# Two graph blocks on one core: the order of instructions at the front, seams and end, and grouped products

## The reference, cut to what matters

```python
h = jnp.maximum(_layernorm(x, axis=-1), 0.0)
x = x + _L0_gnn_ref(h, adj, adj, W_sa, a_sa, W_gcnb, b_gcnb, Wa, ba, Wb, bb)
h = jnp.maximum(_layernorm(x, axis=-1), 0.0)
x = x + _L1_gnn_ref(h, adj, W_stack)

# _L0_gnn_ref(x, ...): one layer
attn_a = sigmoid(concatenate([adj_a @ x, x], axis=1) @ Wa.T + ba)
attn_b = sigmoid(concatenate([adj_b @ x, x], axis=1) @ Wb.T + bb)
h = x @ W_sa
scores = (h @ a_sa[0, :Hd])[:, None] + (h @ a_sa[0, Hd:])[None, :]
e = jnp.where(adj_a != 0, jnp.exp(-leaky_relu(scores, 0.01)), 0.0)
x_a = (e / (jnp.sum(e, axis=1, keepdims=True) + 1e-05)) @ h
x_b = adj_b @ (x @ W_gcnb) + b_gcnb
return sigmoid(attn_a * x_a + attn_b * x_b)

# _L1_gnn_ref(x, ...): two layers of
Wh, Ws = jnp.split(x @ W, 2, axis=-1)
scores = Wh @ Ws.T
a = softmax(scores, axis=-1) * adj
x = leaky_relu(a @ Wh + x, 0.01)
```

## Time and profile before

| what | value |
|---|---|
| median of 3 runs | 1569.0 us (1568.11 to 1570.0) |
| the profiled execution | 1568.53 us |
| its span in the profile | 1566.7 us |
| granted clock of PE, mean | 1.00 |
| instructions | 34636 |
| PE busy | 1533.8 us (98%), 12826 matmuls |
| DVE, ACT, POOL busy | 1130.7 (72%), 1068.2 (68%), 983.9 us (63%) |
| memory traffic | 167.83 MB, mean 107 GB/s |

### The profile page before, as it was taken

One profiled execution on the slowest core, in us unless ns is written; L12 is line 12 of the kernel. 1 busy time (PEld: TensorE's weight loads), 2 busy tenths in 40 slices (PEclk: granted clock), 3 DMA queues, 4 the chain that ended last, 5 costly groups with the idle time before them and its releaser, 6 DMA issues.

```text
span 1566.7 us, 34636 instructions
## 1 busy us (share of the span) xinstructions
PE 1533.8 (98%) x12826; PEld 1524.1 (97%) x12826; DVE 1130.7 (72%) x2119; ACT 1068.2 (68%) x2081; POOL 983.9 (63%) x886
## 2 busy tenths in 40 slices
PE   6999999999999999999999999999999999999998
PEld 5999999999999999999999999999999999999997
DVE  7667666676675677777777777766777777777774
ACT  5689899899984566666666666646666666666666
POOL 4312222222210488888888888847888888888885
PEclk9999999999999999999999999999999999999999
DMA  4354444544440134343433435522443333334343
GB/s 162 65 101 122 116 119 117 149 117 120 116 101 28 42 92 106 107 109 99 107 107 107 111 105 174 183 62 81 104 105 104 104 105 105 104 105 105 105 108 106
DMA packets 98423, 167.83 MB, mean 107 GB/s; under 512 B 15951, under 2 KB 28878, under 8 KB 97998
## 3 DMA queue, kind: packets, MB, share of 16 engines
q1 hardware_dynamic: 70208, 117.75, 27.3%
q0 software_dynamic: 24336, 44.31, 12.0%
q10 hardware_dynamic: 3710, 3.56, 0.7%
HBM read 152.44 MB, written 13.14 MB: 106 GB/s over the span
## 4 chain that ended last, share of the span: by engine, by line
PE 88%; issue 4%; DVE 3%; DMA 2%; POOL 2%; ACT 1%; SPq 0%; DVEq 0%; POOLq 0%; ACTq 0%
PE PS L1349 32%; PE PS L1562 9%; PE PS L1565 9%; PE PS L1564 9%; PE PS L1426 5%; PE PS L1423 5%; PE PS L1425 5%; PE PS L1424 5%; PE PS L1422 5%; POOL FR L541 1%; DMA STGT<-adjt 1%; DMA ROW<-rec_scratch 1%; DMA rec_scratch<-COL 1%; POOL X L534 1%; DVE AF L1158 0%
## 5 line engine op out<-in xcount | busy, mean ns | idle before, releaser
L541 POOL TENSOR_TENSOR FR<-AF,FR 128x512 fp32r<-128x512 f32 x338 | 451.3, 1335 | 124.4 <-ACT FR L752 118.6
L1349 PE MATMUL PS<-FR,RB 128*128 128x256 f32 x3900 | 513.9, 281 | 1.8 <-ACT X L706 1.7
L1349 PEld LDWEIGHTS PS<-FR,RB 128*128 128x128 f32 x3900 | 481.7, 188 | 3.1 <-ACT X L706 3.0
L534 POOL TENSOR_TENSOR X<-X,ROW 128x512 f32<-128x512 f32 x283 | 369.2, 1305 | 81.9 <-ACT ROW L762 81.9
L1562 PE MATMUL PS<-FR,RA 128*128 128x256 f32 x1300 | 370.7, 285 | 3.2 <-POOL FR L541 3.2
L1565 PE MATMUL PS<-FR,RA 128*128 128x256 f32 x1300 | 365.0, 281 | 0.0
L1564 PE MATMUL PS<-FR,RA 128*128 128x256 f32 x1300 | 364.4, 280 | 0.0
L481 POOL DMA_DIRECT2D STGT<-adjt x169 | 91.3, 540 | 298.0 <-PE PS L1426 295.9
L1158 DVE TENSOR_TENSOR AF<-PS,AJ 128x512 f32<-128x512 f32 x338 | 231.1, 684 | 56.1 <-ACT PS L718 46.1
L706 ACT ACTIVATE X<-PS 128x512 f32<-128x512 f32 x272 | 162.5, 597 | 158.8 <-DVE AF L1090 151.4
L1090 DVE TENSOR_TENSOR AF<-PS,AF 128x512 f32<-128x512 f32 x286 | 196.4, 687 | 101.0 <-PE PS L1349 98.6
(11 more groups left out here) (175 smaller groups left out, 2408.1 us busy)
## 6 DMA issues: line engine op xcount, KB each, us to landing
AJ<-adjt SPq DMA_DIRECT2D x338, 256.0 KB, 2.7
STGT<-adjt POOLq DMA_DIRECT2D x169, 256.0 KB, 3.0
xt_scratch<-ROW SPq DMA_DIRECT2D x12, 512.0 KB, 2.6
RB<-xt_scratch SPq DMA_DIRECT2D x12, 512.0 KB, 5.3
x_scratch<-X ACTq DMA_DIRECT2D x13, 256.0 KB, 2.2
ROW<-x_scratch SPq DMA_DIRECT2D x13, 256.0 KB, 3.2
out<-ROW SPq DMA_DIRECT2D x12, 256.0 KB, 3.4
ROW<-rec_scratch SPq DMA_DIRECT2D x22, 128.0 KB, 3.8
```

Of the source, the lines that this page charges most:

```text
L534: nc.gpsimd.tensor_tensor(slot, slot, MB.unsqueeze(1).broadcast_to([P, 2, 256]), ALU.subtract)\
L541: nc.gpsimd.tensor_tensor(LO[g % 2], WA[g % 2], HI[g % 3].bitcast(F32), ALU.subtract)\
L1349: last = nc.tensor.matmul(out, stationary(a, k), moving(b, k), start=(k == 0 and i == 0), stop=(k == K - 1 and i == 2))
```

## The change

It does the following, with names as in the code.

1. unit0: the 20 products come in three groups, eight of adj behind stage_full, eight of e_hi behind hi_done, four of e_lo behind lo_done. weigh and weigh_last: eight products of the high part behind hi_d, four of the low part behind alo_d.
2. Front: transpose0(p+1) runs between products_g(p) and products_h(p) on PE, with new bank turns; ACT, DVE and POOL follow; DVE runs transposed_low(0) before variances, and mask0 before g_low. N_LATE is 27: ACT runs high0 before exp0 in units 14 to 26 too.
3. Seam 1: wh(2) runs before project_q(0) on PE, ACT and DVE; DVE's xt_low(12) comes one step later.
4. The W2 casts move from step 154 to steps 159 and 160.
5. Block 11 leaves NEAR: its reciprocal goes through memory. The layer-2 inputs of blocks 11 and 12 are written in place, so that one store and one load of 512 KB fewer are made.
6. Seam 2: wh(13) to wh(25) use other PSUM banks (WH2_BANK), their evictions on ACT and DVE come a step later (EV_AT), and turn_max(13) comes before the scores.
7. End: block 24's reciprocal is kept and used two steps after its end.

```diff
-N_LATE = UNITS + 1
+N_LATE = 2 * UNITS + 1
+EV_AT |= {182: (13,), 183: (14,), 184: (15, 16, 17, 18, 19, 20), 185: (21,), 186: (22,), 187: (23, 24), 188: (25,)}
+WH2_BANK = (5, 0, 1, 5, 0, 1, 2, 3, 5, 2, 3, 5, 2)
 WH_AT |= {181: (13,), 182: (14,), 183: (15,), 184: (16, 17, 18, 19, 20, 21), 185: (22,), 186: (23, 24), 187: (25,)}
+W2_AT = 159
-NEAR = (PAIRS - 2, PAIRS - 1, LB - 1)
+NEAR = (PAIRS - 1, LB - 1)
+FAR_X2 = PAIRS - 2
-R_END = {v + 3 * (b not in NEAR): b for v, b in A_END.items()}
+R_END = {v + (0 if b == PAIRS - 1 else 2 if b == LB - 1 else 3): b for v, b in A_END.items()}
...
         def turn(pr, i):
-            return 5 * pr + i + 1 if i else max(5 * pr - 4, 0)
+            return 5 * pr + (0, 1, 2, 4, 5)[i] if i else max(5 * pr - 2, 0)
...
                 if S_END.get(v - 2) is not None:
                     keep_max(S_END[v - 2])
-                if A_END.get(v - 1) in NEAR and v - 1 != LAST1:
-                    keep_rec(A_END[v - 1])
-                if x is not None and x < GL:
+                if x is not None and x < GL and x != CH:
                     exponent(x)
                 if e is not None:
                     evict(e)
+                if x == CH:
+                    exponent(x)
                 if x is not None:
                     high(x)
...
-                if v == 154:
-                    dve.wait_ge(w_hi, 4)
+                if v == W2_AT:
+                    dve.wait_ge(w_hi, 3)
                     nc.vector.tensor_tensor(WX[:, 1, :, D:2 * D], MS, WX[:, 0, :, D:2 * D].bitcast(F32),
                                             ALU.subtract).then_inc(wx_ready, 1)
+                if v == W2_AT + 1:
+                    dve.wait_ge(w_hi, 4)
                     nc.vector.tensor_tensor(WX[:, 1, :, 0:D], WRAW1[:, 1, :, 0:D], WX[:, 0, :, 0:D].bitcast(F32),
                                             ALU.subtract).then_inc(wx_ready, 1)
...
             variances(0, 0, 2, 1)
             scales(0, 0, 2)
             normalise(0)
...
             dve.wait_ge(x_in[1], 16)
+            statistics(2, 4)
             statistics(4, 6)
+            transposed_low(0)
             variances(1, 2, 6, 3)
-            transposed_low(0)
             scales(1, 2, 6)
             normalise(1)
...
             xt_low(11)
             wh_low(1)
             post_x1(PAIRS - 1)
+            wh_low(2)
             q_low(0)
             post_norm(PAIRS - 1)
-            wh_low(2)
             post_scales(PAIRS - 1)
             wh_low(3)
             wh_low(4)
...
-                if v == X12_AT:
+                if v == X12_AT + 1:
                     xt_low(PAIRS - 1)
...
+                tiles = [(h, jj, (2 * jj + h) * P) for h in range(2) for jj in range(2)]
+                pe.wait_ge(stage_full[n % NSTG], 16 * (n // NSTG + 1))
+                for h, jj, i0 in tiles:
+                    j, adj, a_to = 2 * u + jj, STG[n % NSTG][:, i0:i0 + P], PS[:, acc(pr) + 2 + h, :]
+                    nc.tensor.matmul(a_to[:, 0:GX], adj, G[:, j, 0:GX], start=(j == 0), stop=False)
+                    nc.tensor.matmul(a_to[:, 0:GX], adj, G[:, j, GX:2 * GX], start=False, stop=(j == T - 1))
+                pe.wait_ge(hi_done, n + 1)
+                for h, jj, i0 in tiles:
+                    j, e_hi, e_to = 2 * u + jj, FR[:, ah(n), i0:i0 + P], PS[:, acc(pr) + h, :]
+                    nc.tensor.matmul(e_to[:, 0:GX], e_hi, RA[:, j, 0:GX], start=(j == 0), stop=False)
+                    nc.tensor.matmul(e_to[:, 0:D], e_hi, RA[:, j, GX:GX + D], start=False, stop=False)
                 pe.wait_ge(lo_done, n + 1)
...
             for p in range(PAIRS):
-                if 1 <= p < PAIRS - 1:
-                    transpose0(p + 1)
                 pe.wait_ge(htlo_done, p + 1)
                 products_g(p)
-                if p == 0:
-                    transpose0(1)
-                    pe.wait_ge(w_ready, 1)
                 if p == 1:
                     turn_left()
+                if p < PAIRS - 1:
+                    transpose0(p + 1)
+                if p == 0:
+                    pe.wait_ge(w_ready, 1)
                 products_h(p)
...
+                pe.wait_ge(hi_d, g + 1)
+                tiles = [(2 * u + h, d, h * 256) for h in range(2) for d in range(K)]
+                for j, d, i0 in tiles:
+                    hi, to = HI[g % 3][:, i0:i0 + 256], PS[:, 4 + b % 2, d * 256:(d + 1) * 256]
+                    nc.tensor.matmul(to, RA[:, j, d * P:(d + 1) * P], hi, start=(j == 0 and d == 0), stop=False,
+                                     skip_group_check=True)
+                    nc.tensor.matmul(to, RA[:, j, D + d * P:D + (d + 1) * P], hi, start=False, stop=False,
+                                     skip_group_check=True)
                 pe.wait_ge(alo_d, g + 1)
...
-                        nc.tensor.matmul(to, w_hi_, hi, start=(u == 0 and h == 0 and d == 0), stop=False,
-                                         skip_group_check=True)
-                        nc.tensor.matmul(to, w_hi_, lo, start=False, stop=False, skip_group_check=True)
-                        last = nc.tensor.matmul(to, w_lo_, hi, start=False, stop=final, skip_group_check=True)
+                for j, d, i0 in tiles:
+                    lo, to = LO[g % 2][:, i0:i0 + 256], PS[:, 4 + b % 2, d * 256:(d + 1) * 256]
+                    last = nc.tensor.matmul(to, RA[:, j, d * P:(d + 1) * P], lo, start=False, stop=(j == T - 1),
+                                            skip_group_check=True)
...
             project_wh(0)
             transpose_x(11)
             project_wh(1)
+            project_wh(2)
             project_q(0)
-            for n in range(2, 6):
+            for n in range(3, 6):
                 project_wh(n)
```

175 lines of the change are left out of this document (83 added, 92 removed).

## The result

The changed kernel takes 1554.67 us at the median of four runs (1553.12 to 1556.08), the kernel before 1568.55 in the runs beside it. The ratio is 0.9916, with a 95% interval of 0.9904 to 0.9928: 13.9 us or 0.84% faster. One execution of e12 took 2744.93 us at a mean granted clock of 0.79 and is left out of its median.

A forecast was written before the change was run, and what follows sets the result against it. PE bounds the kernel, busy 1533.8 of 1566.7 us, so only some 33 us of idling can return. Terms sum to 12.1: 1568.5 - 12.1 = 1556.4, plus 0.5 for the median, 1557; forecast range 1552.5 to 1560.5 (chance 0.55).

The forecast's parts named there:

- Regrouped products: Units and weighs: broken w_hi pairs cost 0, the 676 added waits 0.3 us of loss, ends 0 and 1.7.
- The rule weighed there: Skill's rule that one weight load can serve many products; by it, breaking a pair would cost a load's visible part.
- Front: 0 to about 90 us: g(0) starts earlier, but both orders are level by unit 2; 0, ends -1.5 and +2.
- Units 11 to 16: Late stage load near 102 us: 16 products run before low0(15) is done; 2.0 us gained, upper end 3.6, lower 1.3.
- Seam 1: wh(5) still waits for wh_low(3): 0, ends 0 and 2.1; xt_low(12) a step later gives 0.8, ends 0 and 1.1.
- Weighs that wait for POOL: Four block ends: eight products ahead let POOL's low part come 0.95 us later; 2.6 us gained, ends 1.4 and 3.0.
- W2 casts: Moved to steps 159 and 160, one each: stalls of 0.45 and 0.27 us go; 0.7 gained, ends 0 and 0.7.
- Seam 2: 1030.66 to 1068.96 us: exponents and highs first, evictions later, no stall above 0.3; 5.5 us gained, ends 3.5 and 6.0.
- End: Before 1539.42 us: weighted(24) behind two masks returns about half of 1.8; 0.8 us gained, ends 0.3 and 1.8.
- More: Rival: front's 2, both seam stalls (2.1) and full 3.6 of units 11 to 16 come too; 17.8 us, 1551; chance 0.14.
- The slower one: Rival: breaking 1300 weigh pairs costs; decides from 9.3 ns a pair, at twice that 1581 us; chance 0.07.
- less: Rival: seam 2 gives half (2.8), units 11 to 16 1.3, block ends 1.4; 6.1 us, 1563; chance 0.17.

The follow-up runs named there:

- e12: Changed kernel with old front, wh_low(3) ahead of post_scales, the left-score store cut in two, and the row-maximum fold as a one-operand reduction: 1551.0 us.
- e3: Changed kernel with the front's order and bank turns of before: 1554.8 us, ratio 0.9921 to the kernel before.
- e10: Changed kernel with N_LATE back at 14, so ACT runs exponent before high in units 14 to 26: 1554.83 us, ratio 0.992.
- e6: Changed kernel with weigh and weigh_last in the old order of products behind the low part: 1554.69 us, ratio 0.9921.
- e7: Kernel before with seam 2's part alone (banks, later evictions, turn_max of block 13 first, block 12's reciprocal later): 1562.09 us, ratio 0.997.
- e5: Changed kernel with unit0's 20 products in the old order behind the low part: 1558.88 us, ratio 0.9949.
- e11: Kernel before with the product groups of unit0, weigh and weigh_last alone: 1562.26 us, ratio 0.9963.
- e9: Changed kernel with one more store of left scores (1536 packets of 4 bytes) at unit 60: 1556.03 us in one run.

## Why the prediction was right, and where it wasn't

The forecast was 12.1 us of gain and 1557; measured were 13.9 by the medians and 12.4 between the profiles, inside the forecast's own range. That the total is so near is in part luck. The changed kernel's profile holds 1.55 us at the lower clock and 1.4 us of a long fold, neither of which was in the sum; without them it would have gained about 15 where 12.1 was forecast (the profiles of e3 and e10, which have neither, are 15.1 and 14.9 us under that of before). The block ends were put too high, units 11 to 16, the rest of the first layer and the end too low, and these errors have opposite signs. Point by point:

**Bound.** Right: all that was gained are idle times of PE, at an unchanged price of a product.

**Regrouped products.** The sum had 0 for the pairs and 0.3 for the waits; second-layer groups cost 0.4 to 0.9 in all (0.44 in weighs 170 to 321, nothing in 0 to 150; e6, e7 and the kernels with groups), inside the ends. The rule weighed there doesn't hold here: in the timeline of before, from 1100 to 1500 us, the distance from L1562 to L1564 (same stationary) is 118 ns at the median of 528, and 118 from L1564 to L1565 (new stationary) at that of 529. (The mean of the first is 123.1, since 31 of them, each the first pair behind a turn of a block's end, are 200 to 205 ns long; the new order has 30 such distances from L1575 to L1577.) A repeated stationary is not cheaper. In the first layer the groups gained 0.8 us in 130 units, which no step had; why is open, the runs show only that it comes and goes with the order in unit0.

**Front.** The step gave 0. It costs 1.1 us at unit 10 (e3), and the sum came out right only because the late load swallowed that. I had followed the chain to unit 0 but not the later ones, where the two orders do not level.

**Units 11 to 16.** 2.0 forecast, 1.9 and 2.1 in e5 and e11. The other 1.2 of the 3.1 measured is the front's lateness, counted here instead of there: e3, with the old front, takes 18.72 us from unit 10 to 17.

**Seam 1.** Right: q(0)'s wait goes and wh(5) waits for wh_low(3) instead; 53.7 us in both orders, 0.6 less than before for xt_low(12). The lower clock of some executions, 1.55 us, was in no step.

**Weighs that wait for POOL.** The mis-sized term: 2.6 forecast. Restoring the old order gives 1.97 of stalls back there, of which 1.1 are in seam 2, and so 0.9 for block ends. Only the first of the four places, at 534 to 537, is there in every kernel without groups in weigh. The ones at 740 to 744 and at 976 to 979 are absent from e6 and e7, which have no groups either; ahead of both the trip of the reciprocal through memory was the slowest in the trace of before, 10.3 and 10.1 us (in e7 8.5 and 9.4), which fits, but no run parts it from other causes. (The 0.47 at 969 in e6 is another weigh, 146, behind the moved W2 cast.) The one at 1010 to 1013 stays in e7 and is gone in e6, so that another edit of the change removes it (the W2 casts or block 11; the runs don't part them). And I had costed nothing for what PE's earlier start does to others: with the groups PE and DVE run some 0.5 us further ahead of POOL, so that at block 12 the fold starts inside a POOL instruction. In all ten profiles with grouped weighs and the two-operand fold it has 0.64 to 0.66 us of that instruction ahead of it, and takes 0.92 us in five and 3.42 to 3.44 in the other five; in the three without (before, e6, e7) it starts 0.11 to 0.14 us before the instruction's end and takes 0.41. Two more folds, near 752 in e11 (3.42) and near 755 in e5 (0.92), start 0.64 us before an end as well. The numbers fit a fold that waits: 0.92 is the 0.64 that is left and 0.28, and 3.42 is that and two POOL instructions of 1.25 us from start to start. The Trainium skill ("SBUF — State Buffer", section "SBUF: two separate sides") says that a VectorE operation with two SBUF inputs and a GpSimd operation that reads SBUF exclude each other for the whole instruction. For the fold, the W2 casts (below) and e12 the traces agree; that a waiting fold can lose to the next two POOL instructions as well is measured, not stated there. Not every POOL instruction holds DVE back so: in the first layer low0, with two operands in SBUF, starts inside POOL's root of the layer norm with 0.66 us of it left, eleven times in the trace of before, and takes its usual time:

```profile
119.92 1.15 POOL L486 TENSOR_TENSOR LNT<-LNT,COL 128x2 f32<-128x2 f32 x1 [1.92 <-DVE LNT L905]
120.41 0.68 DVE L967 TENSOR_TENSOR FR<-AF,FR 128x512 fp32r<-128x512 f32 x1
```

What parts the two (the root's 128x2 elements, or its kind) no run shows. Each long fold costs PE about 1.4 us (in the changed kernel 1.08 at L1629 and 0.28 at the turn back).

**W2 casts.** 0.7 forecast, 0.4 measured. The 1.78 us of the second cast is a like case: two operands in SBUF. It is not a matter of the step: at 159 and 160 the two casts take 1.74 and 1.36 us, as they start with 1.19 and 0.81 us of a POOL instruction left, 0.55 us more than that each time, and the POOL instruction behind takes 1.77 in place of 1.3. The first of the two in the changed kernel:

```profile
959.78 1.32 POOL L546 TENSOR_TENSOR FR<-AF,FR 128x512 fp32r<-128x512 f32 x1
959.91 1.74 DVE L1328 TENSOR_TENSOR WX<-ROW,WX 128x512 fp32r<-128x512 f32 x1 [0.63 <-ACT WX L880]
961.04 1.77 POOL L539 TENSOR_TENSOR X<-X,ROW 128x512 f32<-128x512 f32 x1
```

**Seam 2.** 5.5 forecast, 6.0 measured, of them 5.1 by the order and banks alone (e7). The loss itself was 0.2 larger than the 6.0 that the prediction counted, since it took 266 full-size products for 264. The replay found no stall, and there is none. The rival in which half of it comes falls.

**End.** 0.8 forecast, 1.9 measured. Of it 0.4 is the groups' (34.45 in e11 against 34.84; 33.40 in e6 against 32.97), and 1.5 the order's: the term was mis-sized, since I kept weighted(24) ahead of a mask that row_exponent needs. In the new order three masks stand ahead of it, and PE's last transposes wait 0.17.

**Rivals.** "More" came partly true, by the groups' 0.9 in the first layer and the end, not by the front and seam 1 that it named. The slower one, broken pairs, is at most 0.7 ns a pair against the 9.3 from which it decides, 13 times too small. In "less" the parts named add up to 6.1 only if seam 1's 0.8 and the 0.3 for the waits are left out; with them it is 6.6 and 1562.5, which changes nothing here.

## What to carry to other kernels

Order the products of a group by when their operands come, and let each wait only for its own: in weigh it costs 0 to 3 ns a weigh here, and it absorbs what is late by less than the work ahead. But look for what the engine that now runs ahead will meet: here a two-operand operation on DVE slid into a POOL instruction and took back, in five of ten profiled executions, the 1.4 us that the weighs' groups had saved. And where a late transfer sets a time, an edit ahead of it shows nothing, for good or bad; take its cause away or move it first (here a store of 4-byte packets, begun 4 us earlier), then measure the edits.

## What the runs showed of the hardware

A store of 1280 to 1536 packets of 4 bytes holds a 256 KB load beside it for 10.3 to 11.8 us instead of 3.0, at the front and in the first layer's middle (e9). A DVE operation with two operands in SBUF that starts with 0.3 to 1.2 us left of one of POOL's 128x512 subtractions waits for its end (fold 0.92 us, W2 casts 0.85 to 1.78), and can then lose to the next two, 3.42 us in place of 0.41; with 0.14 us or less left it isn't delayed (0.41), beside POOL's 128x2 root neither (0.68), and with one operand in SBUF it ran through (0.70, e12). The granted clock fell to its lower level behind a PE idle of 2.0 us at seam 1 in two executions of seven and cost 1.55 us there; behind the front's idle times it fell in two of eight (0.72 and 0.83 over 25 to 30 us, after and e9), and unit 10 began no later for it (87.04 and 87.65 us, against 87.55 to 87.91 in the other six). What parts the executions where it falls from the others no run shows.
